# Layer 1 of the coupling net in cycles 2 and 3 mixed from two fixed products, with the state left unrotated and the last norm made by token

## The reference

```python
x = x + layernorm(attention(layernorm(x)))      # 16 heads of 8, on the left half of x
x = x + layernorm(ffn(layernorm(x)))

def ffn(x):
    gf = global_net(x.mean(tokens))              # one number per batch
    out = x
    for _ in range(3):
        tf = sigmoid(gelu(gelu(gelu(out @ w1 + b1) @ w2 + b2) @ w3 + b3) @ w4 + b4)   # one number per token
        coupling = 0.1 + adaptive_range * (0.7 * gf + 0.3 * tf - 0.5) * 2
        out = out + coupling * twist(out)
    return out

def twist(x):                                    # quarters of the features
    o_r, o_i, p_r, p_i = split(x, 4)
    return concat([p_r, -p_i, -o_r, o_i])
```

## Time and profile before

| | us |
|---|---|
| median of 3 runs | 3401.14 (3397.94 to 3401.55) |
| profiled execution | 3397.87 |
| its span, first to last instruction | 3396.1 |
| TensorE busy | 3225.2 |
| VectorE busy | 2962.9 |
| ScalarE busy | 2873.4 |
| GpSimd busy | 974.5 |

### The profile page before, as it was taken

The page is one execution under the profiler, slowest core; times in us unless marked ns, Lnnn a source line. Parts: engine busy times, 40 slices in busy tenths (PEclk is TensorE's granted clock), DMA queues, the critical chain, the costliest instruction groups (busy, mean ns, idle before and its releaser), DMA issues.

```text
span 3396.1 us, 56586 instructions
## 1 busy us (share of the span) xinstructions
PE 3225.2 (95%) x19712; PEld 942.6 (28%) x19712; DVE 2962.9 (87%) x5517; ACT 2873.4 (85%) x3812; POOL 974.5 (29%) x1382
## 2 busy tenths in 40 slices
PE   6989999999999999999999999999999999999987
PEld 2222232322323232232322323232232322323223
DVE  7999989898898988989888898988989888898943
ACT  3868979798897979979798897989979798896975
POOL 5012060421505124060421505124060421504015
PEclk7998999999999999999999999999999999999999
DMA  3111111121111112121121111112121121111001
GB/s 89 26 42 43 32 50 33 43 50 43 50 31 50 43 39 54 32 62 32 45 48 45 50 31 47 46 39 54 32 62 32 45 48 45 38 31 51 8 23 38
DMA packets 97500, 144.76 MB, mean 43 GB/s; under 512 B 49472, under 2 KB 60096, under 8 KB 89408
## 3 DMA queue, kind: packets, MB, share of 16 engines
q1 hardware_dynamic: 93520, 123.83, 13.8%
q0 software_dynamic: 3696, 17.31, 2.8%
HBM read 34.61 MB, written 32.51 MB: 20 GB/s over the span
## 4 chain that ended last, share of the span: by engine, by line
PE 61%; DVE 18%; ACT 9%; issue 4%; POOL 4%; SPq 3%; DMA 1%; DVEq 0%; POOLq 0%; ACTq 0%
PE heads_ps L514 24%; PE ring_ps L481 14%; DVE max_parts L974 12%; PE scoresT_ps L499 11%; PE scoresT_ps L602 5%; ACT p_sb L719 4%; DVE stats L985 3%; POOL y_sb L1257 2%; PE scoresT_ps L607 2%; ACT headsT L728 1%; SPq L346 1%; DVE moments L995 1%; POOL rstd L1243 1%; ACT state L790 1%; SPq L321 1%
## 5 line engine op out<-in xcount | busy, mean ns | idle before, releaser
L974 DVE TENSOR_REDUCE max_parts<-ring_ps 128x1 f32<-128x512 f32 x3744 | 2368.5, 683 | 229.2 <-PE ring_ps L481 169.3
L719 ACT ACTIVATE p_sb<-scoresT_ps 128x1024 f32<-128x1024 f32 x2048 | 1970.4, 1024 | 81.3 <-PE scoresT_ps L499 57.4
L481 PE MATMUL ring_ps<-k_rows,q_rows 48*128 48x512 bf16 x3744 | 1085.9, 384 | 33.0 <-DVE max_parts L974 23.6
L514 PE MATMUL heads_ps<-p_sb,v_sb 128*9 128x512 f32 x8192 | 1071.3, 595 | 18.0 <-ACT headsT L728 11.9
L499 PE MATMUL scoresT_ps<-q_rows,k_rows 51*128 51x512 bf16 x4096 | 1021.0, 383 | 7.1 <-ACT p_sb L719 4.3
L481 PEld LDWEIGHTS ring_ps<-k_rows,q_rows 48*128 48x128 bf16 x3744 | 265.4, 94 | 1352.0 <-DVE max_parts L974 1240.7
L1235 POOL CAST max_wide<-max_all 128x16 bf16<-128x16 f32 x128 | 25.1, 196 | 1744.5 <-DVE max_all L980 1744.5
L602 PE MATMUL scoresT_ps<-state,w 128*128 128x512 f32 x732 | 365.9, 623 | 13.0 <-DVE state L1038 12.1
L830 ACT ACTIVATE p_sb<-scoresT_ps,b 128x512 f32<-128x512 f32 x180 | 123.7, 687 | 195.5 <-PE scoresT_ps L602 194.6
L499 PEld LDWEIGHTS scoresT_ps<-q_rows,k_rows 51*128 51x128 bf16 x4096 | 206.7, 93 | 224.5 <-ACT p_sb L719 211.4
L514 PEld LDWEIGHTS heads_ps<-p_sb,v_sb 128*9 128x9 f32 x8192 | 124.3, 88 | 288.5 <-issue 278.1
(11 more groups left out here) (198 smaller groups left out, 2705.0 us busy)
## 6 DMA issues: line engine op xcount, KB each, us to landing
q_rows<-parts SPq DMA_DIRECT2D x744, 32.0 KB
k_rows<-parts SPq DMA_DIRECT2D x744, 32.0 KB
x_sb<-in_x SPq DMA_DIRECT2D x16, 1024.0 KB, 4.9
x_in<-in_x SPq DMA_DIRECT2D x15, 1024.0 KB, 5.4
out<-x_sb SPq DMA_DIRECT2D x15, 1024.0 KB, 3.9
out<-x_in POOLq DMA_DIRECT2D x15, 1024.0 KB, 7.9
q_rows<-max_rows SPq DMA_DIRECT2D x512, 3.0 KB
feat_h<-headsT SPq DMA_DIRECT2D x512, 16.0 KB
```

What stands on the lines that cost most here:

```text
L481: e.matmul(ring_bank(max_taken, u + 1), q_rows[rows, slot, pair, h * BANK + qb * P:h * BANK + (qb + 1) * P], k_rows[rows, slot, pair, kh * ...
L514: m = e.matmul(heads_ps[32 * j:32 * j + DH + 1, :], v_sb[:, b % 2, kb, 4 * (group % NG) + j, 0:DH + 1], p_sb[:, n % 2, j, :], start=(kb == ...
L719: e.activation(p_sb[:, n % 2, 2 * two:2 * two + 2, :].rearrange("p h n -> p (h n)"), scoresT_ps[:, (2 - 2 * two) * BANK:(4 - 2 * two) * BA ...
L974: e.tensor_reduce(max_parts[:, gi % 2, kh, col:col + 1], bank_of(max_taken, u + 1), AX.X, ALU.max).then_inc(max_taken, 1)
```

## The change

`LAYERS` becomes one list of 26 beats. Layer 1 is a product with `state` only in cycle 1. Its result, without bias and gelu, is kept (`plain`). A second product, `OTHER`, multiplies the same state with `w1_turned`, which is w1 with its halves exchanged and signs set so that the product is that of twist(x). Cycle 2's input of gelu is plain + c1 * other; cycle 3's is (plain + c1 * other) + c2 * (other - c1 * plain). These mixes are elementwise operations of 128 x 512 on VectorE and GpSimd (in cycle 3 block m = 0 on VectorE, m = 1 on GpSimd; `draw_plain`, `mix_first` always on GpSimd); `OTHER` holds its ring bank until VectorE has read it. `state` is not changed any more and has one buffer for two.

c1 and c2 are laid with one number per partition (`lay_coupling`, 16 transfers a batch), the last cycle's tanh is made by token with one-column products. In the attention that follows the stage GpSimd makes from these the two factors, the mean and the spread of the result (`finish_tokens`), the turned rows, the norm, the sum and the store (`finish`, at steps 2, 6, 9, 12). The mean of the turned rows comes from `prepare` one attention earlier (steps 20, 24, 28). `turn_back`, `take_back`, the third stats, rstd and norm, `twist`, `update` and `last_half` are gone. `y_sb` has two buffers. The ending starts batch 15's net at beat 34 and its last norm is made by ScalarE, VectorE and GpSimd by token.

```diff
-LAYERS = ((1, 0, 0), (1, 0, 1), (2, 0, 0), (1, 1, 0), (3, 0, 0), (1, 1, 1), (4, 0, 0), (2, 1, 0), (3, 1, 0), (4, 1, 0))
-CYCLE = len(LAYERS)
...
+OTHER = 5
+LAYERS = ((1, 0, 0), (1, 0, 1), (2, 0, 0), (1, 1, 0), (3, 0, 0), (1, 1, 1), (4, 0, 0), (OTHER, 0, 0), (2, 1, 0),
+          (OTHER, 0, 1), (3, 1, 0), (4, 1, 0),
+          (2, 0, 0), (OTHER, 1, 0), (3, 0, 0), (OTHER, 1, 1), (4, 0, 0), (2, 1, 0), (3, 1, 0),
+          (2, 0, 0), (4, 1, 0), (3, 0, 0), (4, 0, 0), (2, 1, 0), (3, 1, 0), (4, 1, 0))
...
-BEAT_UNITS = (4, 1, 2, 1, 2, 1, 2, 2, 1, 1,
-              2, 3, 2, 3, 3, 2, 2, 4, 2, 1,
-              2, 1, 2, 3, 4, 2, 2, 2, 3, 1)
+BEAT_UNITS = (3, 1, 2, 1, 4, 1, 2, 2, 2, 2, 4, 4,
+              2, 2, 3, 2, 3, 2, 4, 2, 4, 3, 3, 2, 3, 2)
...
+STATS0, ROOT0, NORM0, TURN_X = (0, 1, 2, 3), 3, (4, 5, 6, 7), (7, 8)
+PROJECT_QK, SPLIT, PROJECT_V = (14, 16, 18, 21), (16, 18, 20, 23), (20, 24)
-BACK, STATS3, ROOT3, NORM3, ADD_OUT = (8, 9, 10, 11), (10, 11, 12, 13), 14, (16, 17, 20, 24), 26
+NORM1, ADD1, STATS2, ROOT2 = (9, 10, 11, 11), (10, 11, 12, 13), (12, 13, 14, 15), 15
+NORM2, STATE = (18, 19, 20, 21), (22, 23, 24, 25)
...
+DRAW, MIX_OTHER = ((7, 9), (13, 15)), ((9, 11), (15, 17))
+MIX_FIRST, TAKE_FIRST = ((8, 10), (14, 16)), ((9, 11), (15, 16))
+TURN, MIX_SECOND, TAKE_SECOND = (17, 21), (18, 22), (18, 22)
+FINISH, PREPARE = (2, 6, 9, 12), (20, 24, 28)
...
+SHIFT = 34
...
+END_NORM1, END_ROOT2, END_NORM2, END_STATE = (18, 18, 19, 20), 22, (25, 25, 26, 26), (30, 31, 32, 33)
+END_PREPARE, END_FINISH = 28, 30
...
+            def lay_coupling(b, j):
+                cycle, c = cycle_of(j), LAYERS[j][1]
+                if b >= 2:
+                    e.wait_ge(out_stored, 16 * (b - 1))
+                e.wait_ge(coupled, 4 * b + 2 * cycle + c + 1)
+                for t in range(TPH):
+                    at = c * TPH + t
+                    e.dma_start(c_token[:, b % 2, cycle, at:at + 1],
+                                couple[0:1, c, t * P:(t + 1) * P]).then_inc(c_laid[c], 16)
...
                 if layer == 1:
-                    if cycle == 0:
-                        e.wait_ge(state_ready, 4 * (b + 1))
-                    else:
-                        e.wait_ge(state_a_done[k], 4 * before + 2 * cycle - 1 + c)
-                        e.wait_ge(state_b_done[k], 4 * before + 2 * cycle - 1 + c)
+                    e.wait_ge(state_ready, 4 * (b + 1))
                     for f in range(2):
...
+                if layer == 4 and cycle == 2:
+                    for u in range(2):
+                        for s in range(2):
+                            rows = slice(64 * s, 64 * s + 64)
+                            o = e.matmul(layer_bank(j, s)[:, u:u + 1], hidden3[rows, c, u * P:(u + 1) * P],
+                                         w4[rows, :], start=True, stop=True)
...
+            def other_product(b, c, m):
+                ps = ring_bank(other_mixed, mix_count(b, c, m), float("inf"))
+                for f in range(2):
+                    o = e.matmul(ps, w1_turned[:, f, m * P:(m + 1) * P], state[:, f, c * BANK:(c + 1) * BANK],
+                                 start=(f == 0), stop=(f == 1))
+                o.then_inc(other_done, 1)
...
+                    e.activation(plain[:, 2 * c + m, :], ps, ACT.Copy).then_inc(plain_kept, 1)
...
+            def take_first_mix(b, c, m):
+                e.wait_ge(first_mixed, mix_count(b, c, m))
+                e.activation(hidden1[:, 2 * c + m, :], mixed[:, 2 * c + m, :], ACT.Gelu,
+                             bias=b1[:, m:m + 1]).then_inc(mix_act, 1)
...
+            def draw_other(b, c, m):
+                e.wait_ge(coupled, 4 * b + c + 1)
+                e.wait_ge(other_done, mix_count(b, c, m))
+                e.tensor_tensor(mixed[:, 2 * c + m, :], bank_of(other_mixed, mix_count(b, c, m)), couple[:, c, :],
+                                ALU.mult).then_inc(other_drawn, 1)
+            def mix_other(b, c, m):
+                e.wait_ge(plain_drawn, mix_count(b, c, m))
+                e.tensor_tensor(other[:, 2 * c + m, :], bank_of(other_mixed, mix_count(b, c, m)), other[:, 2 * c + m, :],
+                                ALU.subtract).then_inc(other_mixed, 1)
+            def draw_second(b, c, m):
+                e.wait_ge(coupled, 4 * b + 2 + c + 1)
+                e.wait_ge(other_mixed, mix_count(b, c, m))
+                e.tensor_tensor(other[:, 2 * c + m, :], other[:, 2 * c + m, :], couple[:, c, :],
+                                ALU.mult).then_inc(second_drawn[m], 1)
+            def mix_second(b, c, m):
+                e.wait_ge(first_mixed, mix_count(b, c, m))
+                e.wait_ge(second_drawn[m], 2 * b + c + 1)
+                e.tensor_tensor(other[:, 2 * c + m, :], other[:, 2 * c + m, :], mixed[:, 2 * c + m, :],
+                                ALU.add).then_inc(second_mixed[m], 1)
...
+            def mix_first(b, c, m):
+                e.wait_ge(other_drawn, mix_count(b, c, m))
+                e.wait_ge(plain_kept, mix_count(b, c, m))
+                tile = mixed[:, 2 * c + m, :]
+                e.tensor_tensor(tile, tile, plain[:, 2 * c + m, :], ALU.add).then_inc(first_mixed, 1)
+            def draw_plain(b, c, m):
+                e.tensor_tensor(other[:, 2 * c + m, :], plain[:, 2 * c + m, :], couple[:, c, :],
+                                ALU.mult).then_inc(plain_drawn, 1)
...
+            def finish_tokens(b):
+                tok = lambda i: token[:, i, :]
+                c1, c2 = c_token[:, b % 2, 0, :], c_token[:, b % 2, 1, :]
+                for c in range(2):
+                    e.wait_ge(c_laid[c], 2 * 16 * TPH * (b + 1))
+                e.wait_ge(hid_done, ITEMS * (b + 1))
+                e.tensor_scalar(tok(2), t_token[:, b % 2, :], ar_token[:, 0:1], shift[b % 2][:, 0:1], ALU.mult, ALU.add)
...
+                finished(e.tensor_tensor(tok(11), tok(5), minus_half[:, :], ALU.pow))
+                e.tensor_tensor(tok(3), tok(3), tok(11), ALU.mult)
+                e.tensor_tensor(tok(7), tok(7), tok(11), ALU.mult)
+                finished(e.tensor_tensor(tok(4), tok(4), tok(11), ALU.mult))
+                e.tensor_scalar(tok(8), tok(7), -1.0, None, ALU.mult)
+                finished(e.tensor_scalar(tok(12), tok(4), -1.0, None, ALU.mult))
...
+            def finish_turned(b):
+                y, quarter = y_of(b), D // 2
+                plus = token[:, 4, :].unsqueeze(2).to_broadcast([P, NT, quarter])
+                minus = token[:, 12, :].unsqueeze(2).to_broadcast([P, NT, quarter])
+                e.tensor_tensor(turned[:, :, 0:quarter], y[:, :, 2 * quarter:3 * quarter], plus, ALU.mult)
+                e.tensor_tensor(turned[:, :, quarter:2 * quarter], y[:, :, 3 * quarter:E], minus, ALU.mult)
+                e.tensor_tensor(turned[:, :, 2 * quarter:3 * quarter], y[:, :, 0:quarter], minus, ALU.mult)
+                finished(e.tensor_tensor(turned[:, :, 3 * quarter:E], y[:, :, quarter:2 * quarter], plus, ALU.mult))
...
+            def finish_rows(b):
+                y = y_of(b)
+                for t in range(NT):
+                    m = e.tensor_scalar(y[:, t, :], y[:, t, :], token[:, 3, t:t + 1], token[:, 8, t:t + 1], ALU.mult, ALU.add)
...
+            def finish_sum(b):
+                y = y_of(b)
+                for i in range(4):
+                    rows = slice(2 * i, 2 * i + 2)
+                    m = e.tensor_tensor(y[:, rows, :], y[:, rows, :], turned[:, rows, :], ALU.add)
...
+                e.dma_start(out_dram[b], y, accum_op=ALU.add).then_inc(out_stored, 16)
...
+            def prepare(b, i):
+                y, quarter = y_of(b), D // 2
+                plus = scratch[:, 0, :].rearrange("p (t e) -> p t e", t=NT)
+                minus = scratch[:, 1, :].rearrange("p (t e) -> p t e", t=NT)
+                if i == 0:
+                    e.wait_ge(norm_act[2], 4 * (b + 1))
+                    e.tensor_tensor(plus, y[:, :, 2 * quarter:3 * quarter], y[:, :, 3 * quarter:E], ALU.subtract)
+                    finished(e.tensor_tensor(minus, y[:, :, quarter:2 * quarter], y[:, :, 0:quarter], ALU.subtract))
+                if i == 1:
+                    finished(e.tensor_tensor(plus, plus, minus, ALU.add))
+                    finished(e.tensor_tensor(plus[:, :, 0:32], plus[:, :, 0:32], plus[:, :, 32:64], ALU.add))
+                if i == 2:
+                    for width in (16, 8, 4, 2, 1):
+                        finished(e.tensor_tensor(plus[:, :, 0:width], plus[:, :, 0:width], plus[:, :, width:2 * width],
+                                                 ALU.add))
+                    e.tensor_scalar(turned_mean[:, b % 2, :], plus[:, :, 0], 1.0 / E, None, ALU.mult).then_inc(mean_ready, 1)
...
+                    if j == END_PREPARE:
+                        for i in range(3):
+                            prepare(b, i)
+                        end_turned_rows(b)
+                    if j == END_FINISH:
+                        for i in range(4):
```

(1 more changed line is left out.)

711 lines of the change are left out of this document (363 added, 348 removed).

## The result

| kernel | median, us | lowest to highest | ratio to before, 95% interval |
|---|---|---|---|
| before | 3401.4 | 3397.9 to 3406.3 | |
| changed | 3603.8 | 3599.4 to 3604.6 | 1.0586 [1.0572, 1.0599] |
| forecast | 3340 | 3290 to 3405 | |

The forecast had the wrong sign, and the time is 199 us above the top of its range.

What follows compares the result with a forecast made beforehand. It took TensorE to bound the coupling stage after beat 6, VectorE close behind, and ScalarE the attention. 3397.87 - 59 (14 stages x 4.2) + 1 (ending) = 3340 us; range 3290 to 3405.

Steps and rivals of the forecast that it cites:

- TensorE is the limit there: Coupling stage after beat 6: TensorE busy 53.7 of 57.3 us was said to set its length, VectorE close behind.
- I put every beat from 7 to 25 at the dearer of the two engines: After beat 6: each beat costed at the larger of TensorE's and VectorE's time; nineteen maxima summing to 48.4 us.
- I take 52: After beat 6: the summed beats, scaled by VectorE's busy account to 52 to 53 us, taken as 52.
- 53.1: Predicted length in us of the part after beat 6, new waits included, for 57.3 before: 4.2 gained per stage.
- I take 1.1; bounds 0 and 8: New waits for mixes, tightest at beats 15 to 19: 1.1 us a stage; upper bound four waits of 2 us.
- Rival C: Coupling stage: mixes hang on GpSimd, four waits of 2 us with in-order TensorE; slower, 3438 us; chance 0.13.
- The two locked engines: Second mixes: by the SBUF rule VectorE and GpSimd could lose 0.5 us each, 2 a stage, 28 in all.
- The counts of work: Coupling stage: TensorE busy about 59 us, VectorE about 60, GpSimd 4 less than before, ScalarE about 6 less.
- The attention: GpSimd's finishing work moved into attention costs nothing; attention stays 130 to 131 us; SyncE's 16 extra issues also 0.
- The ending: After the last attention: batch 15 starts 3 us earlier, engines stand 15 us for the shift; net +1, between -10 and +8.
- my three terms, 13, 5 and 14: Ending, from shift to last tanh: 13 us to cycle 1's first layer 4, 5 of mixing, 14 more; given as 33.
- The clock: Ending: TensorE's halved clock after the stand costs 1 us, from one case in the trace that cost 1.6.

Runs made afterwards that it cites:

- b1: Kernel before, layer-1 products of cycles 2 and 3 without their second K block (7.65 us of TensorE less a stage): 3381.8 us, ratio 0.9940.
- f3: Kernel before, GpSimd's twist made twice in four places of a stage and in the ending: 3470.6 us, ratio 1.0197.
- e3: Changed kernel, ScalarE's gelus of cycles 2 and 3 read the plain product and wait for no mix, mixes still made: 3427.5 us, ratio 1.0067.
- e8: Changed kernel with gelus reading the plain product, and VectorE's twelve mixing operations on 64 of 512 columns: 3392.1 us, ratio 0.9961.
- f1: Changed kernel with gelus reading the plain product, plus one extra TensorE product at beats 12, 17, 19, 23: 3466.6 us, ratio 1.0185.
- e1: Changed kernel, VectorE runs a beat's mixes before that beat's maxima instead of behind them: 3521.7 us, ratio 1.0341.
- h1: Kernel before with only the last sum and norm made by token in the next attention; layer 1 still from the rotated state: 3389.8 us, ratio 0.9959.
- e2: Changed kernel, TensorE makes 1, 2, 3 and 3 extra products ahead of the waits at beats 12, 17, 19, 23: 3565.6 us, ratio 1.0470.
- e4: Changed kernel, GpSimd's eight split subtractions of a coupling stage on 64 of 512 columns: 3600.1 us, ratio 1.0571.
- e9: Changed kernel with mixes before maxima, and second half's cycle-2 layer 4 one beat ahead of first half's cycle-3 layer 2: 3497.2 us, ratio 1.0292.
- b2: Kernel before, layer 1 of cycles 2 and 3 takes its second K block first, each block waiting for its own update: 3402.6 us, ratio 1.0000.

## Why the prediction was wrong, by its steps

**"TensorE is the limit there."** Refuted (b1). That an engine is 94 to 96% busy in a stretch, as TensorE is in the earlier trace rows, shows that it has little idle time, not that the stretch shrinks with its work. Taking 7.65 us of it shortened a stage by 1.0 to 1.5. TensorE, VectorE and the chain were tied: in the kernel before, 1.3 us more on GpSimd at each of four places in the chain cost 4.1 a stage (f3); in e3, 5.4 less on VectorE gave 1.8 (e8) and 3.8 more on TensorE cost 2.9 (f1).

**"I put every beat from 7 to 25 at the dearer of the two engines" and "I take 52".** This step failed first. With every wait for a mix gone (e3) the part after beat 6 takes 56.2 in the mean, 4.2 above the 52 and 3.1 above the 53.1 with my waits in it; beats 0 to 6, which I left alone, add 1.1. Over 14 stages that is 57 of the 87 us between 3340 and 3427; 24 more lie in the attentions that begin at a lower clock and 6 in the ending. A maximum per beat assumes that both engines enter each beat together and that an operand is ready when its beat comes.

**"I take 1.1; bounds 0 and 8."** The larger miss: about 14 a stage (69.9 against 56.2). I added up GpSimd's durations from the moments to the last operand, 10.9 us, and let VectorE's share take its own 0.6. But an operand's delay is that of the queue it stands in: five reduces, then four, and the stand of VectorE itself. e1 shows the place. I also took the four waits as additive, 2 us each in the bound. The two followed above feed each other through the ring, and each is followed by products at half clock. None of that is in a price per wait. Rival C had the waits of an in-order TensorE, and neither their size nor, for the most part, their engine: it hung them on GpSimd's queue.

**The two locked engines.** The prediction left out of its sum the 2 us a stage that the rule would cost. VectorE's draw with both operands in SBUF takes 1.28 in the mean where the one that reads PSUM takes 0.68; GpSimd's beside it 1.45 where 1.27 is usual.

```profile
L1075 DVE TENSOR_TENSOR p_sb<-p_sb,couple 128x512 f32<-128x512 f32 x32 | 41.0, 1282 | 8.5 <-ACT couple L860 8.5
...
L1064 DVE TENSOR_TENSOR headsT<-ring_ps,couple 128x512 f32<-128x512 f32 x48 | 32.7, 682 | 11.7 <-PE ring_ps L677 11.7
```

The Trainium skill, "SBUF — State Buffer", section "SBUF: two separate sides", has a VectorE operation with two inputs in SBUF and a GpSimd one that reads SBUF take a shared port in turn, the second waiting for the whole of the first; the trace agrees, since the long draws stand beside GpSimd's own draw or mix of block 1, L1378 and L1383 (the one at 929.77 took 1.73). It costs 0.6 for each of two draws a stage, in the tightest place of the chain.

**The counts of work** were right: VectorE 60.8 a stage where about 60 was said, GpSimd 44.7 (47.2 less 2.5; I said 4), ScalarE 49.9 (4.6 less; I said 6). TensorE 70.5 and not 59: the work is gone, the clock took it back (24.9 us of each stage stand at the lower level, which makes at most 12.4 us of it).

**The attention**, costed at nothing with GpSimd's finish and prepare in it: right in the changed kernel, 130.7 for 130.2, and 130.3 in h1; what attentions add in e2 to e4 and e9 goes with the clock at their start. From the second headsT copy on, an attention has the pace of before. SyncE's sixteen small issues: no cost seen in h1 either.

**The ending.** The gap was foreseen at 15 us, ended by the shift: 13.1 on ScalarE and 10.4 on TensorE. The price was not: +10 for +1. Batch 15's state did not come 3 us earlier (61.3 after the last headsT copy, 60.3 before); from the shift to the last tanh it took 38.7 us, not 33 (my three terms, 13, 5 and 14, add to 32), with layer-2 products at 3.65 and 3.75.

**The clock.** I had put 1 us for it, in the ending alone, from one case. The layer-2 products at 917.60 and 934.79 took 3.75 each, behind 3.44 and 5.10 of waiting. The mean granted clock of 0.930 over 3602 us is some 500 us at the lower of its two levels (twice 0.070 x 3602); before, 0.985, some 100. The Trainium skill, "TensorE: Matmul & The Clock Gate", section "What's actually happening", has idleness halve the clock; the trace agrees, at the places named.

**What stays open:** how the loss divides between the stand and the half clock behind it; how much of the first mixes' 42 us is GpSimd's rstd chain; whether `NORM0` a beat earlier is what lengthens beats 0 to 6, since no run moves it alone; why some attentions begin at a lower clock (24 of the 30 us by which e3's traced span exceeds that of the kernel before lie there, its stages being as long); and what latency alone costs in the kernel before, since f3 held VectorE up too and b2 moved an operand that was not late.
